# A pipelined attention, memory and routing kernel: the rest of a batch in new ticks, the softmax sums in another bank with a reciprocal in four parts, and the key and value product directly in front of a weighing

## What is computed

```python
# 1: 16 query heads of 32 share one key head and one value head
K = ctx @ Wk + bk;  V = ctx @ Wv + bv                 # 2048 x 32 each
scores = einsum('bhqd,bkd->bhqk', layernorm(x) @ Wq + bq, K) * 32 ** -0.5
x = x + softmax(scores) @ V (heads side by side) @ Wo + bo
# 2: a delta-rule memory, 4 heads of 128, chunks of 64: A = inv(I - A0), ...
x = x + memory(layernorm(x), Ww, Wr, decay, log_alpha)
# 3: top-1 mixture of 16 experts, at most 128 rows each
idx = argmax(softmax(layernorm(x) @ Wg));  loc = running count of that expert
h = relu(dispatched @ w1[e]);  out = (h @ w2[e])[idx, loc] * gate
x = x + out where loc < 128
```

## Time and profile before

| | |
|---|---|
| median of 3 runs | 2451.77 us (2449.37 to 2453.38) |
| the profiled execution, its own time | 2450.42 us |
| its span, first to last instruction | 2448.6 us |
| PE, DVE, ACT, POOL busy | 91%, 56%, 49%, 67% of the span |
| mean granted TensorE clock | 0.939 |
| first and last start of the sums (L392) | 167.7 us (batch 0), 1950.8 us (batch 15) |
| first instruction of the expert stage on PE | 2027.8 us |

### The profile page before, as it was taken

The page is one execution under the profiler, slowest core; times in us unless marked ns, Lnnn a source line. Parts: engine busy times, 40 slices in busy tenths (PEclk is TensorE's granted clock), DMA queues, the critical chain, the costliest instruction groups (busy, mean ns, idle before and its releaser), DMA issues. The chain is left out here.

```text
span 2448.6 us, 34965 instructions
## 1 busy us (share of the span) xinstructions
PE 2217.4 (91%) x12608; PEld 1425.3 (58%) x12608; DVE 1366.6 (56%) x2263; ACT 1198.8 (49%) x2237; POOL 1638.1 (67%) x1323
## 2 busy tenths in 40 slices
PE   5879898989898989898989898999898768999999
PEld 3426464646464646464645464645454447999998
DVE  3656666666666666666666666656665433333333
ACT  3646464646464646464645455555554313333333
POOL 0677777777777777777777777767777714555654
PEclk8889999989998999998989898989898778999999
DMA  4631111111111111111111112121102009999995
GB/s 176 216 95 53 57 48 57 48 56 48 57 48 57 58 53 59 57 48 57 48 60 49 61 44 65 40 65 39 44 5 82 18 5 365 343 365 354 354 365 191
DMA packets 108156, 263.74 MB, mean 108 GB/s; under 512 B 9849, under 2 KB 35065, under 8 KB 99792
## 3 DMA queue, kind: packets, MB, share of 16 engines
q1 hardware_dynamic: 98448, 235.32, 27.4%
q10 hardware_dynamic: 5952, 14.29, 1.7%
q0 software_dynamic: 3584, 11.90, 1.2%
HBM read 223.74 MB, written 25.72 MB: 102 GB/s over the span
## 5 line engine op out<-in xcount | busy, mean ns | idle before, releaser
L913 POOL TENSOR_TENSOR psum<-psum,p 128x512 f32<-128x512 f32 x896 | 1156.0, 1290 | 360.2 <-ACT p L550 265.8
L705 DVE TENSOR_REDUCE mpart<-bank 128x1 f32<-128x512 f32 x1024 | 680.4, 685 | 398.7 <-PE bank L355 392.8
L550 ACT ACTIVATE p<-bank 128x512 f32<-128x512 f32 x1024 | 594.4, 599 | 597.4 <-PE bank L368 588.2
L368 PE MATMUL bank<-qT,kT 97*128 97x512 f32 x1024 | 501.2, 491 | 4.6 <-ACT p L550 4.5
L355 PE MATMUL bank<-kT,qT 96*128 96x512 f32 x1024 | 490.6, 481 | 10.7 <-DVE mpart L705 7.8
L355 PEld LDWEIGHTS bank<-kT,qT 96*128 96x128 f32 x1024 | 206.2, 201 | 264.5 <-issue 148.7
L380 PE MATMUL bank<-p,v 128*32 128x512 f32 x2048 | 309.1, 679 | 1.2 <-ACT p L550 1.0
L368 PEld LDWEIGHTS bank<-qT,kT 97*128 97x128 f32 x1024 | 206.2, 202 | 149.7 <-issue 112.8
L1155 POOL TENSOR_TENSOR w2l<-w,w2h 128x1024 fp32r<-128x1024 f32 x64 | 203.2, 3176 | 75.3 <-PE ebank L1070 54.5
L330 PE MATMUL bank<-cst,w_first 128*128 128x128 f32 x1024 | 155.2, 275 | 13.6 <-DMA w_first<-in_ctx 13.3
L579 ACT COPY cxT<-bank 128x512 f32<-128x512 f32 x256 | 150.0, 588 | 12.9 <-PE bank L330 12.8
(11 more groups left out here) (159 smaller groups left out, 3083.5 us busy)
## 6 DMA issues: line engine op xcount, KB each, us to landing
w<-in_w SPq DMA_DIRECT2D x48, 2048.0 KB, 20.2
w_first<-in_ctx SPq DMA_DIRECT2D x64, 1024.0 KB, 5.0
w_first<-in_w SPq DMA_DIRECT2D x16, 2048.0 KB, 12.4
dispatched<-route ACTq DMA_DIRECT2D x17, 513.0 KB, 4.8
dis<-dispatched SPq DMA_DIRECT2D x16, 513.0 KB, 3.6
qT<-qh SPq DMA_DIRECT2D x128, 64.0 KB, 2.0
xin<-in_x SPq DMA_DIRECT2D x16, 256.0 KB, 2.6
qT<-qs SPq DMA_DIRECT2D x64, 64.0 KB, 2.0
```

Of the source, the lines that this page charges most:

```text
L368: e.matmul(B_BANK[u % 2][:], kT[b % 2][0:3 * HD + 1, k * P:(k + 1) * P], qT[b % 2][0:3 * HD + 1, g * 512:(g + 1) * 512], start=True, stop= ...
L550: e.activation(p[n % NP][:], B_BANK[u % 2][:], ACT.Exp).then_inc(p_act.sem, 1)
L705: e.tensor_reduce(mpart[g % 2][:, n:n + 1], A_BANK[(17 * g + n) % 2][:], AX.X, ALU.max).then_inc(max_dve.sem, 1)
L913: e.tensor_tensor(acc[:], first[:], p[(UNITS * b + u) % NP][:], ALU.add).then_inc(psum_pool.sem, 1)
```

## The change

The ticks of `finish` move: the sums from 4 to 9, the reciprocal becomes four of 128x128 at ticks 9 to 12, `att` goes from 5 to 13, x1 from 8 to 15, and all that follows by 5 to 7 ticks, except `eg`, `oh`, `loc` and `row`, of which the last two go from 118 and 120 to 123 and 125. The sums are issued directly behind the weighing of tick 9 and write the denominators to `KV_BANK` instead of `PV_BANK`; the weighing waits only for ACT's copy of `PV_BANK`, and the first product of keys and values for the last reciprocal. `KV_AT` moves from ticks 23, 39, 55, 71 to 25, 41, 57, 73, which are ticks of a weighing, and stands directly in front of it. Queries go from tick 27 to 30 and are sent three ticks later; the turns of the values stay at ticks 46 and 78.

```diff
-NORM, XN, XNT, QPROJ, QSEND = 1, 5, 10, 27, 38
+NORM, XN, XNT, QPROJ, QSEND = 1, 5, 10, 30, 41
 TILE_AT = [8 + 4 * k for k in range(KB)]
-KV_AT = [TILE_AT[4 * c + 3] + 3 for c in range(4)]
-VT_AT = [KV_AT[2 * m + 1] + 7 for m in range(2)]
+KV_AT = [TILE_AT[4 * c + 3] + 5 for c in range(4)]
+VT_AT = [KV_AT[2 * m + 1] + 5 for m in range(2)]
-POST = dict(xb=2, sums=4, att=5, x1=8, x1_add=11, norm2=12, xn2=15, ss=16, x12=17, rn=17, xn2T=18, rk=20, V=21,
-            V_copy=24, rkT=28, I=32, XT1=34, X1=39, Vn=93, oT2=96, x2=99, x2_add=102, store=103, norm3=103, xn3=106, xn3T=109,
-            lg=112, eg=113, oh=114, loc=118, row=120)
-LEVEL_AT = [[42 + 9 * n, 45 + 9 * n, 48 + 9 * n] for n in range(LEVELS)]
+POST = dict(xb=2, sums=9, recip=[9, 10, 11, 12], att=13, x1=15, x1_add=18, norm2=19, xn2=22, ss=23, x12=24, rn=24,
+            xn2T=25, rk=27, V=28, V_copy=31, rkT=34, I=38, XT1=40, X1=44, Vn=98, oT2=101, x2=104, x2_add=107,
+            store=108, norm3=108, xn3=111, xn3T=115, lg=118, eg=119, oh=120, loc=123, row=125)
+LEVEL_AT = [[47 + 9 * n, 50 + 9 * n, 53 + 9 * n] for n in range(LEVELS)]
...
-        o_dve = named("o_dve", "recip att")
+        o_dve = named("o_dve", "recip0 recip1 recip2 recip3 att")
...
-                    e.wait_ge(*(oS_act.at(b, g - 1) if g else o_dve.at(b - 1, "recip")))
+                    e.wait_ge(*(oS_act.at(b, g - 1) if g else oS_act.at(b - 1, HG - 1)))
...
-                for out, lhs, src in ((PV_BANK, cst[:, C_ONES, 0:HD], psum), (P_BANK, cst[:, C_STACK, 0:HD], oS)):
+                if b + 1 < B:
+                    e.wait_ge(*kvs_dve.at(b + 1, 3))
+                for out, lhs, src in ((KV_BANK, cst[:, C_ONES, 0:HD], psum), (P_BANK, cst[:, C_STACK, 0:HD], oS)):
...
-                    if c or b:
-                        e.wait_ge(*(kvs_dve.at(b, c - 1) if c else kvs_dve.at(b - 1, 3)))
+                    if c:
+                        e.wait_ge(*kvs_dve.at(b, c - 1))
+                    elif b:
+                        e.wait_ge(*(o_dve.at(b - 2, "recip3") if b > 1 else kvs_dve.at(0, 3)))
...
-                if t == POST["sums"]:
-                    if b == 0:
-                        e.wait_ge(*const_in.at(CONSTS - 1))
-                    sums(b)
...
                     if quad:
                         weigh(*quad)
+                    if i >= 1 and t == POST["sums"]:
+                        sums(i - 1)
...
-                if t == POST["sums"]:
+                if t in POST["recip"]:
+                    h = POST["recip"].index(t)
                     e.wait_ge(*sums_pe.at(b))
-                    e.reciprocal(recip[:], PV_BANK[:]).then_inc(o_dve.sem, 1)
+                    e.reciprocal(cut(recip, h), cut(KV_BANK, h)).then_inc(o_dve.sem, 1)
                 if t == POST["att"]:
-                    e.wait_ge(*o_dve.at(b, "recip"))
+                    e.wait_ge(*o_dve.at(b, "recip3"))
```

## The result

The changed kernel takes **2492.51 us** (median of 4 runs, 2489.3 to 2497.2) against 2451.22 us of the kernel before on the same chip. The ratio is **1.017, 95% interval 1.0157 to 1.0183**: slower by some 41 us, where 2413 us was forecast and 2451 us was the upper end of the range.

What follows compares the result with a forecast made beforehand. PE's work was taken to bound the middle of an iteration, with losses around the batch boundary. 2.0 - 0.2 + 0.8 = 2.6 us a batch, 15 times = 39 us, less 0.2, gave 2413 us; range 2382 to 2451.

Steps and rivals of the forecast that it cites:

- gain 2.0 us a batch: Addition into `route` to x1: x1 starts 0.8 us earlier and PE has 1.2 us more work done, together 2.0.
- at least 23.1 + 1.5 = 24.6 us: Route to x1: DVE's stretch without waits, 23.1 us, plus 1.3 for two maxima and 0.2 for the reciprocal's extra starts.
- (c): Tick 9: DVE waits 1.6 us for a weighing, both halves of the sums and the maximum's product.
- (a): DVE's wait between `lg` and `oh`: 2.19 us go, about 0.6 for gate product and exponential stay.
- (b): Ticks 120 to 122: DVE waits 1.4 us for the new group's first products while PE weighs at the lower clock.
- -0.2: x1 to V: new 1.2 us wait for `mneg` at tick 24, old waits of 0.98 us covered; loss 0.2 a batch.
- If `ss` holds the copies: x1 to V: ACT's copies queued behind `ss` were counted as covered; if the cover is gone, another -1 a batch.
- +0.8 a batch: Key and value product beside a weighing: 0.2 us saved on each of four products a batch (ends 0.4 and 1.6).
- The split reciprocal: DVE's reciprocal in four parts, route to x1: three more starts cost +0.2 us.
- Slower: Rival, chance 0.15: pause before x1 over 5 us, lower clock one period longer; -1.1 us a batch, 2468 us.
- The wait only moves: Rival, chance 0.25: DVE makes PE wait at ticks 2 to 8, 30.6 us to x1; 0.6 a batch, 2443 us.
- More: Rival, chance 0.15: clock stays up, `att` after 27.2 us, narrow products change freely; 4.8 us a batch, 2380 us.

Runs made afterwards that it cites:

- f13: e1 with three short DVE instructions of `row` as one-tensor instructions with one-column operands: 2442.48 us, ratio 0.9974.
- e12: e8 with three short DVE instructions of `row` as one-tensor instructions with one-column operands: 2401.01 us, ratio 0.9793.
- e1: Changed kernel with key and value products back at ticks 23, 39, 55, 71, turns of the values at 46 and 78: 2466.39 us, ratio 1.0062.
- e8: Changed kernel with ACT's two key copies six ticks behind their product instead of two, DVE's low part eight instead of four: 2440.49 us, ratio 0.9959.
- e7: e1 with the reciprocal whole (128x512 at tick 9) instead of in four parts: 2463.25 us, ratio 1.0057.
- e6: e1 with POOL adding only 8 of 512 columns for the last four units of each batch: 2402.38 us, ratio 0.981.

## Why the prediction was wrong, step by step

**The boundary, "gain 2.0 us a batch".** The failed step here is the bound "at least 23.1 + 1.5 = 24.6 us": it took `row` at its old 2.35 us. Moved to tick 125 its thirteen instructions run beside POOL's adds, and took 4.26 us in two batches of three. In the trace of the kernel before one of them, L840, already took 0.68 us beside an add, where its neighbour L842 took 0.16; I read 2.35 us as a property of the instructions. With the stretch comes PE's wait of 2.85 us, the lower clock over the weighing and the sums, and DVE's 4.08 us behind them, where (c) said 1.6. Measured 30.6 us from route to x1, forecast 28.6. With the one-tensor forms route to x1 takes 28.6 us (f13 in every batch, e12 in the mean), which is the number of the forecast, but in part by luck: DVE's waits there are 0.8 us for (a), 1.5 for (c) where 1.6 stood, and none for (b), where 1.4 stood; in its place DVE waits 1.49 us for POOL's `rs` in front of the next batch's layer norm, which the forecast didn't have. That the wait for POOL would go and that for `att` stay was right; the latter is 2.3 us in each batch, below the 3 to 4.5 named, and PE waits 2.9 us a batch for maxima in the same stretch. The sign of being wrong that the prediction named, the lower clock over ticks 0 to 9, was there (0.55 around the sums).

**x1 to V, "-0.2".** The new wait for `mneg` was forecast at 1.2 us and is 0.9 (13.6 us in 16 times). The wait before V went. "If `ss` holds the copies" didn't happen.

**The product beside a weighing, "+0.8 a batch".** The price itself was right: 4 x 0.20 to 0.27 = 0.8 to 1.1 us for 0.8. Its sign, a weighing 1.7 to 1.8 us behind the product's start, did not come (1.87): the saving lies on either side of the pair. The second failed step is that the part was priced on PE alone. I listed the queries, the store and the scatter as moved at nothing, but not ACT's key copies, which follow the product by two ticks and so passed in front of the copy of X, whose place moved from tick 39 to 44 while the product went from 39 to 41. From I to Vn this cost 3.1 us a batch instead of a gain: 2.6 of waits and 1.4 of lower clock, less what the placing and the missing tick gave. Of the total, taking the part back gives 26 us (e1) and late key copies give 52 (e8); since they give 49 with the product back too, leaving them out was wrong for the moved rest already. How much of this is the queue order behind the moved product, and how much DVE's low part and the clock, stays open.

**The rivals.** *Slower* had 0.15 and the right sign, and its mark (x1 later than 31.5 us) is met in five of the twelve batches, with the lower clock over the sums that it named. But its own path, a pause of over 5 us before x1, did not come (2.3 us), and it knew neither `row`'s stretch nor ACT's queue. *The wait only moves* described ticks 2 to 8 rightly; its 30.6 us to x1 is the number measured, by luck, since it had `row` at 2.35 us. *More* was wrong.

**The split reciprocal** was priced at +0.2 us a batch and nothing else, 3 us in all; e7 bears this out.

## What to carry to other kernels

When a step is moved, list what follows it on every other engine at a fixed distance, and for each such instruction what it now passes on its own in-order queue: here two copies that wait, with the subtraction on DVE that follows them, cost more than the move could gain, and four ticks more for them gave 52 us. A duration read from a trace belongs to its neighbours too: in this kernel a short VectorE instruction with two tensors from SBUF took 0.16 to 0.22 us between GpSimd's adds and up to 1.17 us beside them, so look whether such chains can stand where GpSimd pauses, or be written with one tensor and one-column operands. And a product that is moved for its own sake may have been the cover of a wait behind it.

## What the runs showed of the hardware

VectorE instructions that read two tensors from SBUF wait for a GpSimd add that is running: 128x16 in 0.88 us for 0.16, one column in 0.98 for 0.16 and in 1.17 for 0.22 (after against e6), while one-tensor forms of the same one-column sums take 0.21 to 0.27 beside the same adds (e12), and the reduction of 128x512 from PSUM stays at 0.63 to 0.69. The Trainium skill, "GPSIMD Engine Reference", section "Specifications", says that GpSimd shares its SBUF interfaces with VectorE and that instructions with two SBUF inputs contend; the trace agrees. How long one waits depends on where the add stands at its start. In the changed kernel every long L834, L843 and L848 began within an add of 1.27 us and ended 0.01 to 0.04 us behind its end, having begun 0.4 to 0.9 us into it (L834), 0.31 (L843) and 0.10 (L848); L845, which also read two tensors, began between two adds and took 0.16 in each batch. In the kernel before, L840 began 0.60 us into an add and took 0.68, and that too ended 0.02 behind the add. One tensor is no safe form by itself: L829, a `tensor_scalar` of 128x16, takes 1.17 us beside the adds, in e12 as well, and 0.23 in the last batch, where none runs.
